# Attention with its keys as a ring of four tiles: 16 slots a batch instead of 20, and new tables for everything between

## The reference, cut to what matters

```python
# B, S, D = 8, 512, 256; 16 heads of 16; experts: E = 64, top 8, capacity 256, inner size 128
h   = layernorm(x) * (1 + ca) + sa
qkv = h @ w_qkv + b_qkv
band = abs(i - j) <= 64                                  # each query sees the keys 64 to either side
a   = softmax(q @ k.T * 16 ** -0.5 + where(band, 0, -inf)) @ v
x   = x + ga * (a @ w_out + b_out)
h   = layernorm(x) * (1 + cb) + sb
x   = x + gb * moe(h)          # scores, 4 of 8 groups, 8 experts a token, silu(g) * u, scatter back
```

## Time and profile before

| | before |
|---|---|
| median of 3 runs | 906.13 us (905.16 to 908.19) |
| the profiled execution: its own time | 907.57 us |
| its span | 905.8 us |
| PE busy | 681.8 us, 75% |
| DVE, ACT, POOL busy | 478.9, 394.4, 509.8 us |
| first slot of batch 0 to the end of batch 7's last slot | 55.8 to 522.6 us |
| first load of the experts' rows | 613.5 us |

### The profile page before, as it was taken

How to read it: one execution, slowest core, us unless ns; L and a number is a source line. 1 busy time by engine, 2 the same in 40 slices (tenths; PEclk the granted TensorE clock), 3 DMA queues, 4 the chain that set the end, 5 groups by cost and what they waited for, 6 DMA issues and landing times.

```text
span 905.8 us, 15461 instructions
## 1 busy us (share of the span) xinstructions
PE 681.8 (75%) x4760; PEld 466.9 (52%) x4787; DVE 478.9 (53%) x1964; ACT 394.4 (44%) x876; POOL 509.8 (56%) x519
## 2 busy tenths in 40 slices
PE   5679899999999999999797942006999888888000
PEld 3335556556566565565455522005888777676000
DVE  3065559869698697786787736201222222222048
ACT  2336566657566566665644511002444333334000
POOL 4000002057577476575767767772788888888810
PEclk9869999999999999999989975557999999999555
DMA  8684896748757577373536794107999998898997
GB/s 325 164 339 164 276 354 211 245 139 271 266 172 259 175 257 254 117 237 123 191 120 182 210 292 120 28 4 224 274 288 266 266 175 160 162 159 160 204 307 318
DMA packets 168334, 191.47 MB, mean 211 GB/s; under 512 B 22137, under 2 KB 150677, under 8 KB 168252
## 3 DMA queue, kind: packets, MB, share of 16 engines
q1 hardware_dynamic: 132220, 134.15, 46.6%
q0 software_dynamic: 30336, 38.03, 20.1%
q10 hardware_dynamic: 5696, 18.30, 5.3%
HBM read 100.64 MB, written 110.67 MB: 233 GB/s over the span
## 4 chain that ended last, share of the span: by engine, by line
PE 47%; POOL 14%; DMA 11%; DVE 10%; issue 9%; ACT 6%; ACTq 1%; SPq 1%; POOLq 0%; DVEq 0%
POOL acc_d L832 8%; PE outT L1171 7%; DMA acc_d<-ys,xg 7%; POOL slots_d L746 5%; PE scoresT L1394 5%; PE scoresT L1151 4%; PE stageA L1092 4%; PE scores L1129 4%; PE scoresT L1155 4%; PE stageA L1110 3%; PE stageC L1212 3%; ACT PT L890 2%; DMA Qs<-MT 2%; DVE junk L1453 2%; PE turns L1181 2%
## 5 line engine op out<-in xcount | busy, mean ns | idle before, releaser
L746 POOL DMA_INDIRECT slots_d<-H,dest x256 | 260.8, 1019 | 155.2 <-issue 87.9
L832 POOL DMA_INDIRECT acc_d<-ys,xg x124 | 191.6, 1545 | 55.0 <-issue 29.2
L1453 DVE CUSTOM_DVE_ANT_0 junk<-scores,mask 128x256 bf16<-128x256 f32 (+1 forms) x512 | 170.9, 387 | 72.1 <-PE scores L1129 70.8
L890 ACT ACTIVATE PT<-scoresT 128x512 f32<-128x512 f32 (+1 forms) x320 | 150.5, 509 | 47.5 <-PE scoresT L1155 45.6
L1394 PE MATMUL scoresT<-xgT,wgu 128*128 128x256 f32 x512 | 125.5, 388 | 17.5 <-ACT xgT L1005 17.4
L1151 PE MATMUL scoresT<-mask,identb 128*128 128x512 bf16 (+1 forms) x320 | 110.3, 345 | 18.7 <-ACT PT L890 14.5
L1394 PEld LDWEIGHTS scoresT<-xgT,wgu 128*128 128x128 f32 x512 | 95.4, 192 | 40.8 <-ACT xgT L1005 27.9
L1155 PE MATMUL scoresT<-Qs,Ks 98*128 98x256 bf16 (+1 forms) x640 | 110.9, 255 | 0.0
L1129 PE MATMUL scores<-Ks,Qs 96*128 96x256 bf16 (+1 forms) x512 | 93.7, 266 | 4.0 <-DVE mrowmax L1453 1.8
L1155 PEld LDWEIGHTS scoresT<-Qs,Ks 98*128 98x128 bf16 x640 | 64.0, 100 | 38.2 <-issue 8.6
L1171 PE MATMUL outT<-PT,Va 128*32 128x256 f32 (+1 forms) x1280 | 80.4, 356 | 1.8
(11 more groups left out here) (260 smaller groups left out, 1059.9 us busy)
## 6 DMA issues: line engine op xcount, KB each, us to landing
xg<-slots_d SPq DMA_DIRECT2D x64, 324.0 KB, 4.0
slots_d<-blank ACTq DMA_DIRECT2D x26, 648.0 KB, 5.2
parts_d<-parts SPq DMA_DIRECT2D x32, 384.0 KB, 3.4
Qs<-parts_d SPq DMA_DIRECT2D x96, 128.0 KB
Ks<-parts_d SPq DMA_DIRECT2D x90, 128.0 KB
acc_d<-zero SPq DMA_DIRECT2D x32, 272.0 KB
wgu<-L_ffn_w_gate_dram SPq DMA_DIRECT2D x64, 128.0 KB, 3.6
wgu<-L_ffn_w_up_dram SPq DMA_DIRECT2D x64, 128.0 KB, 3.7
```

What stands on the lines that cost most here:

```text
L746: pool.indirect_dma_start(out=slots_d[:, :], in_=H2[bt.par][:, t, :], in_offset=None, out_offset=bass.IndirectOffsetOnAxis(ap=dest[bt.par] ...
L832: pool.indirect_dma_start(out=acc_d[ACC[e]][:, :], in_=ys[e % NY][:, h, :], in_offset=None, out_offset=bass.IndirectOffsetOnAxis(ap=xg[e % ...
L890: sc_.activation(PT[m % NPT][:, :, 0:w], src, ACT.Exp).then_inc(sems["exp"], 1)
L1453: ins = v.tensor_tensor_reduce(out=junk[:, i, lo:hi], in0=bS[n % 2][:, i * 2 * P + lo:i * 2 * P + hi], in1=mask[:, lo:hi], scale=1.0, scal ...
```

## The change

The keys are stored as before, but behind the last key the first 64 keys are copied again, by a new POOL piece `ring` in two halves of 8 heads each. Tile u now starts at key 128u + 64, so four tiles hold all 512 keys, and the last holds the last and the first 64. It meets the last and the first 128 queries, with a mask of its own (`ends`), in two products instead of one. `U` is 4, a batch has 16 slots, all exponentials are 512 wide, `values` come at u = 2 (tiles 0, 1) and u = 0 (2, 3), and `turn_m` stands between the two pairs of slot u = 2. All tables are new.

```diff
-U = T + 1
+U = T
 AT = dict(
-    load_x=(-14,),
-    stats=(-15, -11),
-    a_rstd=(-10,),
-    a_norm=(-8,),
+    load_x=(-12,),
+    stats=(-10, -8),
+    a_rstd=(-12,),
+    a_norm=(-5,),
...
-    stack=(8, 13),
+    stack=(6, 11),
...
+    ring=(11, 15),
 BEHIND_IT = dict(
-    op=(4, 6),
-    x1=(4, 6),
+    op=(2, 3),
+    x1=(2, 3),
...
-    stats2=(5, 6),
-    c_rstd=(5, 6),
-    xhat=(6, 7),
-    norm2=(6, 8),
+    stats2=(3, 3),
+    c_rstd=(3, 3),
+    xhat=(3, 5),
+    norm2=(5, 5),
 SECOND = dict(
-    stack=(9, 14),
+    stack=(8, 10),
-SENDS = sends_from(22, (1, 2, 2, 2, 1, 2, 1, 2, 2, 1, 2, 2, 2, 1, 2, 1, 2, 2, 1, 1))
+SENDS = sends_from(19, (1, 1, 3, 0, 3, 1, 2, 3, 2, 2, 1, 3, 3, 2, 2, 3, 0))
...
-        FILLS = {3: [0, 1], 4: [2, 3], 0: [4, 5], 1: [6, 7], 2: []}
+        FILLS = {2: [0, 1], 3: [2, 3], 0: [4, 5], 1: [6, 7]}
...
+            def ring(bt, half):
+                after(pool, "qk_ld1" if half else "qk_ld", bt, 192)
+                heads = slice(half * H // 2, (half + 1) * H // 2)
+                gp.tensor_copy(Ks[bt.par][0:MROW, heads, BAND + S:KW], Ks[bt.par][0:MROW, heads, BAND:2 * BAND]
+                               ).then_inc(sems["ringed"], 1)
...
-                w = P if u in (0, U - 1) else 2 * P
-                src = bST[m % 2][:, 0:2 * w].rearrange("p (h q) -> p h q", h=2)
-                sc_.activation(PT[m % NPT][:, :, 0:w], src, ACT.Exp).then_inc(sems["exp"], 1)
+                src = bST[m % 2][:, :].rearrange("p (h q) -> p h q", h=2)
+                sc_.activation(PT[m % NPT][:, :, :], src, ACT.Exp).then_inc(sems["exp"], 1)
...
+                if u == U - 1 and p == 0:
+                    after(pe, "ringed", bt, 2 * g // QUADS + 1)
...
-                    ready = [(now, g, 0), (now, g, 1), (now, g, 2)] if u == 3 else []
+                    ready = [(now, g, 0), (now, g, 1)] if u == 2 else []
...
+                        if p == 0 and u == 2 and (g < QUADS - 1 or nxt):
+                            turn_m(*((now, g + 1) if g < QUADS - 1 else (nxt, 0)))
```

More of the change, by code:

```diff
@@ L113 @@
     x1_store=(11,),
-    xs=(10,),
+    xs=(9,),
     stats2=(4, 5),
     c_rstd=(5, 5),
[L117 to L123, removed]
+    xhat=(5, 7),
+    norm2=(5, 7),
+    h2T=(7, 9),
+    lg=(9,),
+    route=(10, 10, 11, 11, 11, 12, 12, 12, 12, 12, 13, 14),
+    cnt=(15,),
+    key=(12,),
 )
@@ L130 @@
     x1=(4, 5),
-    x1_store=(10,),
-    xs=(8,),
+    x1_store=(8,),
+    xs=(7,),
     stats2=(4, 6),
[L134 to L141, removed]
+    c_rstd=(5, 5),
+    xhat=(5, 7),
+    norm2=(6, 7),
+    h2T=(8, 8),
+    lg=(9,),
+    route=(9, 9, 9, 9, 10, 10, 12, 12, 12, 14, 14, 14),
+    cnt=(15,),
+    key=(15,),
 )
@@ L147 @@
     stats=(0, 0),
-    a_rstd=(3,),
+    a_rstd=(4,),
     a_norm=(2,),
-    a_mod=(2,),
+    a_mod=(0,),
     hT=(3, 4),
[L152 to L155, removed]
-    stack=(9, 14),
-    v=(13, 14),
-    wrap=(5,),
+    proj=(5, 5, 7, 7),
+    sub=(6, 6, 6, 6, 8, 8, 9, 9),
+    part=(5, 5, 6, 6, 6, 6, 7, 7, 8, 8, 9, 9),
+    store=(6, 7, 10, 10),
+    stack=(8, 10),
+    v=(9, 9),
+    wrap=(6,),
+    ring=(11, 13),
 )
@@ L576, in body @@
                         load_x(bt)
-                    if not prev and slot == 13:
+                    if not prev and slot == 10:
                         store_mod()
@@ L602, in early_w @@
                 after(sp, "exp", now, 2 * slot)
[L603 removed]
+                for n in range((slot - 1) * WEIGHTS_BEHIND // (SLOTS - 1), slot * WEIGHTS_BEHIND // (SLOTS - 1)):
+                    load_w(slice(n, n + 1), n)
             def store_x1(bt):
@@ L753, in send_some @@
                 for n, i in enumerate(rows):
[L754 to L757, removed]
+                    after(pool, "exp", now, 2 * slot + min(n, 1))
                     send(bt, i)
@@ L766, in body @@
                         wrap(bt)
+                    for bt, half in steps("ring", now, slot):
+                        ring(bt, half)
                     for bt, half in behind("c_rstd", now, slot):
@@ L803, in _ @@
             wrap(batch(0))
+            ring(batch(0), 0)
+            ring(batch(0), 1)
             batches(body)
@@ L1263, in body @@
                             values(*tile, p)
-                    if u == 2 and ahead[0]:
-                        turn_m(*ahead)
                     for bt, k in steps("hT", now, slot):
```

105 lines of the change are left out of this document (54 added, 51 removed).

## The result

The changed kernel took 950.97 us in the median of 4 runs (945.74 to 955.82), the kernel before 907.15 in 4 (905.16 to 908.19): a ratio of 1.0482, interval 1.0454 to 1.051. That is 43.8 us slower, where 7.9 were forecast.

A forecast was written before the change was run, and what follows sets the result against it. PE bounded the batches before; with the change POOL's loop would, at 62.0 us in batches with 32 sends. With batch 0 and batches 6 to 7 this summed to +7.4 us: 914 us, own range 909 to 922, overall 891 to 927.

The forecast's parts named there:

- PE gains nothing by wider products: Merging two 256-column mask products into one of 512 on PE saves nothing: 0.11 us each against 0.22.
- The stand on POOL, 8 to 13 us: In batches 2 to 5 POOL's queue stands at `a_rstd` in slot 4, waiting 8 to 13 us for DVE's `stats`.
- The ring takes 62.0 us: Loop POOL, ACT, PE, DVE, POOL through `a_rstd` and 31 sends: 62.0 us a batch, bounds 57.6 and 65.7.
- So in the batches with 32 sends POOL takes over from PE: POOL's loop, no longer PE's work, sets these batches, each 3.3 us longer than in the kernel before.
- Batch 1 keeps 58.7: the same PE work, its waits put elsewhere: Batch 1, which has no sends, stays at 58.7 us.
- Batch 0 at 62.0: Batch 0 grows 3.3 us from 58.7: PE waits 4.1 us for the keys' load, with longer lower clock.
- Batch 6 to 7, 54.8 us, and 26.7 to the first send: From slot 5: 39 sends, copies and `c_rstd` to batch 7, then logits and 17.7 us to batch 6's first send.
- The tail the same: Behind batch 6's first send the same queue follows; the delayed `c_rstd`, 3.8 us, is hidden by sends.
- The third rival, the maxima's DMA: `turn_m` has two slots instead of three: up to 1.8 us a quad in every batch, 920 to 930; chance 0.12.
- the stand costs little: Rival: DVE reaches the second `stats` early, POOL's loop turns at its least, 57.6 us; 893 to 896, chance 0.28.
- PE, 3 us or more at a mask product: Sign in the profile after: PE waits this long for the exponential, and the clock dips once a batch.
- theory A: The forecast's account: POOL's wait at `a_rstd` closes a loop that sets the batches, at 61 to 64 us; chance 0.43.

The follow-up runs named there:

- e14: e11 with the last of the four projections in slot 7 instead of 6, its parts and `sub` moved later too; 915.42 us.
- e11: The changed kernel with the edits of e1, e2, e5, e6, e9 and e10 together; 918.74 us.
- e1: The changed kernel with `a_rstd` in slot 9, behind both halves of `stats`, instead of slot 4; 953.17 us.
- e2: The changed kernel with batch 5's sends beginning in slot 0 of batch 7, not slot 14 of batch 6; 948.09 us.
- e16: The changed kernel with e2's sends and e10's loosened tables for batches 5 and 6 alone; 942.17 us.
- e9: The changed kernel with the edits of e1, e2, e5 and e6, and `turn_m` behind the second pair of its slot; 925.78 us.
- e5: The changed kernel with the edits of e1 and e2, and DVE's routing steps spread over more slots; 935.88 us.
- e6: The changed kernel with e1's and e2's edits, first `xhat` half in slot 4 instead of 3, one `sub` and its part in 6 instead of 5; 933.63 us.
- e10: The changed kernel with the edits of e1, e2, e5 and e6, and the tables of batches 5 and 6 loosened; 923.66 us.
- e12: The kernel before with four `route` parts in slot 15 and the first `xhat` half in slot 5 instead of 6; 920.70 us.

## Why the prediction was wrong

The sign was right, mostly for another reason. By the forecast's own steps:

- *PE gains nothing by wider products*: right or nearly. PE's busy time for batches 1 to 5 at full clock is 275.4 us before, 274.5 in e14 and 271.5 in e11, so at most 4 us of 275. ACT's saving was a sum of durations, 11.4 us; its busy time in exponentials, which overlap in pairs, fell from 150.4 to 147.5.
- *The ring's copies, 0.8 us each*: 0.63.
- *The stand on POOL, 8 to 13 us*: right (11.0 to 14.5). *The ring takes 62.0 us*: nearly right in size where it closes, 63.5 and 64.6 in the change. PE and DVE took 15.6 us of it from slot 5 to the second moments in batch 4, forecast 13.3, with one of PE's new waits (1.21 us) and a lower clock in it. **"So in the batches with 32 sends POOL takes over from PE" is the step that failed.** It set the ring against a PE loop of 58.7 us, as long as before. PE's loop had itself become 63 to 65 us, so the two were level: the ring held PE up by 1.5 us in all, and e1 took it away without gain.
- *"Batch 1 keeps 58.7: the same PE work, its waits put elsewhere"*: the same error in the open. The work was the same, and the waits were not put elsewhere but added: 5.5 to 7 us a batch instead of 2.5 to 3 (waits over 0.25 us), and some 1.7 us of slower work behind them. From the order of the instructions I had read where POOL's steps went, and not what stands on DVE ahead of slot 13's maxima, or on ACT ahead of slot 4's exponentials. Batches 1 to 5 came out at 316.2 us; by the forecast's ring they would be about 307.
- *Batch 0 at 62.0*: 64.5, with waits for ACT's parts (1.65 and 1.59 us) and DVE's `on` (2.20), none for the keys. The term had the right sign and the wrong cause.
- *Batch 6 to 7, 54.8 us, and 26.7 to the first send*: mis-sized by 9.9 and 7.3. The first cost is the early first send (6.35 us of POOL's queue, some 4.6 of the time) and, not split further, the lower clock and PE's new waits in batch 7, the second the packed tables of the last batches; e2 and e16 give 3 and 9 us of it back.
- *The tail the same*: 5.4 us longer. 2.4 of it is the first expert (below); the rest I did not pin down. In e1 to e9, with the same program behind the send, it took 380.2 to 385.1 us, and 380.1 in the kernel before, so most of it does not hang on the tables.

The third rival, the maxima's DMA, did not decide: its waits inside the change's batches are 0.8 to 1.7 us, at most one in a batch, and e9, which starts that DMA later still, gained 3 us. The rival "the stand costs little" was right in that one thing for the middle batches, and wrong on its mechanism (DVE did not reach the second `stats` early, it took 15.6 us instead of 11.4) and its time.

Of what was to be seen, POOL's wait and its sends came as listed, and the dips of the clock. The starts of batches 3 to 5 lie 63.9 and 65.1 us apart, 61 to 64 were forecast. ACT waited for `nmean` in six places but in batches 3 to 5 for the landing. "PE, 3 us or more at a mask product" did not come there: 1.5 to 2.4. That sign, with the `c_rstd` row that waits for DVE, told against theory A before any run was made. That the time came out slower, as forecast, is in the main luck.

What is shown: the placements cost time by themselves (e5, e6, e9, e10, and e12 in the old kernel), and taking the stand away gains nothing in the change as it is, while putting it back costs 6 to 10 us once they are loosened, most of it in batch 6. That the lower clock follows from the waits is argued from where it falls, since no run changes the clock alone. Not shown either is whether the 5 us that e14 still loses in batch 7 are placements too.

## What to carry to other kernels

When a hand-written order is packed into fewer slots, check the critical engine's loop first: for each product that needs another engine's result, list what now stands ahead of that result in the other engine's queue. A stall on another engine, however long, counts only from the point where its queue comes through later than the one it feeds; look at what ended the wait at the next hand-over, and count the landing of the queue's last transfer to the queue. And test a suspected ring from both sides, once with less on it and once with more: two level rings answer the first with nothing and the second nearly in full.
